# Lane 1's input product made by ScalarE and TensorE, both output products by GpSimd, in a selective-scan recurrence

## The chip, the cores and the metric

The kernel runs on one core of a Trainium2 chip. The metric is the device time of one launch in microseconds; lower is better.

## What is computed

Six sublayers of a post-norm decoder on x (4, 512, 128), each followed by a residual add and a LayerNorm: a long convolution (`hyena`), a masked cross attention (`cross0`), a quantised MLP (`bitffn`), a selective scan (`scan`), a cross attention with 16 heads (`cross1`) and a product-key mixture of 1024 experts (`experts`). The change touches the fourth, whose core is:

```python
u, res = split(x @ W_in)                       # (B, 512, 256) each
u = silu(u)
delta = softplus(u @ W_delta + b_delta)        # (B, 512, 256)
Bm = u @ W_B;  Cm = u @ W_C                    # (B, 512, 16) each
A = -exp(A_log)                                # (256, 16)
def step(h, inp):                              # over the 512 positions
    d_t, B_t, C_t, u_t = inp
    h = exp(d_t[..., None] * A) * h + d_t[..., None] * B_t[:, None, :] * u_t[..., None]
    return h, einsum('bdn,bn->bd', h, C_t)
y = (scan(step, 0, ...) + u * D_param) * silu(res)
return y @ W_out
```

For each state n of 16 and each sequence this is: an input product delta*u*B_n, a decay exp(delta*A_n), a first-order scan along the 512 positions, an output product h*C_n, and a sum over n.

## The kernel before

A hardware loop of two iterations takes two sequences each. The two are the *lanes* s = 0 and 1; each has its own arena in SBUF (`mem`, carved into tiles by `per_lane`) and its own four PSUM banks `ps[:, 0..3, :]`. Every engine has one program per sublayer and lane, written as a generator that yields stage numbers; `in_turn` merges the two lanes' generators by taking the smaller stage next, lane 0 first when equal. What comes out is one fixed instruction order for each engine. An engine that waits for a semaphore holds back all that stands behind it in this order; within one lane and engine the order is always that of the code. `w.next(G(name, s), k)` waits until the named semaphore has been raised k more times, `.then_inc` raises it, `w.link` waits for the engine's own instruction.

The recurrence holds its 256 channels as two halves of 128 partitions (DJ = 2), the 512 positions along the free dimension, so a tile of one n is 128 x 1024. Lane by lane, for n = 0 to 15:

- ScalarE (L964): the decay dA for n, two exponentials of 128 x 511; from n = 2 on after scan n - 2.
- TensorE (L682): B_n broadcast over the partitions into bank 0 by a matmul with `row_pick`, C_n likewise into bank 3. For this VectorE has split B and C into three bf16 parts (`BCS`, L1236 to L1240).
- VectorE, stage 4 + n (L1259): input product dBu = DU * B_n; stage 4.2 + n (L1267): the scan into HS or TU by turns.
- The output product HC: in lane 0 (`POOL_LANE = 0`) ScalarE copies C_n to SBUF (`CSB`) and GpSimd multiplies (L1479); in lane 1 VectorE multiplies (L1277).
- TensorE, stage 4.5 + n (L703): the sum over n, two matmuls with the identity that accumulate HC into banks 1 and 2.

Ahead of it lie, in stage 2, the products for delta (L671) and for B and C (L676), ScalarE's softplus as Abs, Exp (L952) and Ln (L955), and VectorE's delta (L1251) and DU = delta * u (L1254). Behind it lie VectorE's L1282 and L1286 (skip term and gate) and the output matmul (L710). GpSimd otherwise only makes the small inverse square roots (L1463) and, in the preparation, constants: among them `row_pick` (L362, L364), which stand ahead of `p_const`, for which TensorE's first matmul (L382) waits beside all the early loads (`p_load`, issued on SP and on ScalarE's queue). `bitffn`'s L1177 squares x on VectorE. SP's program only loads and stores.

Of the kernel before, what the change touches and what calls it, by code (L numbers as in the profile page):

```python
# [19 lines left out]
ALU = mybir.AluOpType  # L20
# [38 lines left out]
def decoder(nc, x, ctx_1024, mask_BxSxS2_ik1, L0_attn_w_in, L0_attn_b_in, L0_attn_w_conv,  # L59
# [28 lines left out]
    POOL_LANE = 0  # L88
# [3 lines left out]
    h_pad = nc.dram_tensor("h_pad", (3 * P,), F32, kind="Internal").ap()  # L92

    with ExitStack() as ctx:
# [18 lines left out]
        row_pick = sb("row_pick", [96, 2 * NS, P], BF16)  # L113
# [69 lines left out]
        WORDS = 12600  # L183
# [20 lines left out]
        def per_lane(**sizes):  # L204
# [16 lines left out]
        TU, TR, UU, SPA, SPE, DL, DU, BCS, BC1, BCM, dBu, HS, HC = per_lane(  # L221
            tu=(P, (DJ, S), F32), tr=(P, (DJ, S), F32), uu=(P, (DJ, S), F32), spa=(P, (DJ, S), F32),
            spe=(P, (DJ, S), F32), dl=(P, (DJ, S), F32), du=(P, (DJ, S), F32), bcs=(96, (S,), BF16),
            bc1=(2 * NS, (S,), F32), bcm=(2 * NS, (S,), BF16), dbu=(P, (DJ, S), F32), hs=(P, (DJ, S), F32),
            hc=(P, (2, DJ, S), F32))

        _, CSB = per_lane(front=(P, (7 * DJ * S + S // 2,), F32), csb=(P, (S,), F32))

        _, dA = per_lane(front=(P, (3 * DJ * S,), F32), da=(P, (2, DJ, S), F32))


# [39 lines left out]
            silu_r d_ready bc_ready ln_ready delta_ready bcs_ready B_ready C_ready dA_ready  # L271
            dbu_done scan_done hc_done y_acc yg_ready k_ready ksq_ready kn_ready kT_ready v_ready
            v_sb qsq_ready ssq_ready ssq_sb aq_sb s_drained xr_ready sim_ready sim_sb wh_ready wh_used
            z_ready g_sb hw_ready hwT_ready aq_ready own_done pn_ready wT_ready ssq_turned eo_ready eo_drained asum_ready c_sb softplus_step""".split()
# [64 lines left out]
        with nc.Block() as block:  # L339
# [15 lines left out]
            def _(pool):  # L355
# [6 lines left out]
                w.link(nc.gpsimd.memset(row_pick[:], 0.0))  # L362
                for g in range(3):
                    w.link(nc.gpsimd.affine_select(  # L364
                        out=row_pick[:], in_=row_pick[:], compare_op=ALU.not_equal, fill=1.0,
                        base=-2 * NS * g, pattern=[[-1, 2 * NS], [0, P]], channel_multiplier=1))
# [164 lines left out]
        def body(it):  # L531
            with nc.Block() as block:  # L532
                @block.sync
                def _(sp):
                    for s in range(LANES):
# [6 lines left out]
                                     .rearrange("o (k p) c -> p (o k) c", p=P)).then_inc(sg["mask_loaded"][s], 16)  # L542
                    for s in range(LANES):
# [13 lines left out]
        def pe_program(block):  # L557
            @block.tensor
            def _(pe):
# [96 lines left out]
                def scan(s):  # L656
# [23 lines left out]
                    def broadcast(row_n, bank, ready):  # L680

                        pe.matmul(ps[:, bank, :], row_pick[:, row_n, :], BCS[s][:], start=True, stop=True)\  # L682
                            .then_inc(G(ready, s), 1)

                    yield 3
                    w.next(G("bcs_ready", s))
                    w.next(G("delta_ready", s))
                    broadcast(0, 0, "B_ready")
                    broadcast(NS, 3, "C_ready")
                    for n in range(NS):  # L690
                        yield 4.1 + n
                        if n + 1 < NS:
                            w.next(G("dbu_done", s))
                            broadcast(n + 1, 0, "B_ready")
                        yield 4.5 + n
                        if n + 1 < NS and s == POOL_LANE:
                            w.next(G("c_sb", s))
                            broadcast(NS + n + 1, 3, "C_ready")
                        w.next(G("hc_done", s))
                        if n + 1 < NS and s != POOL_LANE:  # L700
                            broadcast(NS + n + 1, 3, "C_ready")
                        for j in range(DJ):
                            mm = pe.matmul(ps[:, 1 + j, :], ident[:], HC[s][:, n % 2, j, :],  # L703
# [824 lines left out]
```

## Time and profile before

| | us |
|---|---|
| median of 3 runs | 1267.41 |
| lowest and highest | 1264.33, 1274.64 |
| span of the profiled execution | 1266.5 |

| engine | busy us | share of the span | instructions |
|---|---|---|---|
| PE (TensorE matmul) | 885.7 | 70% | 3174 |
| DVE (VectorE) | 988.6 | 78% | 1819 |
| ACT (ScalarE) | 570.6 | 45% | 1593 |
| POOL (GpSimd) | 256.6 | 20% | 125 |

The two recurrences lie at 181 to 305 us and at 793 to 916 us. DVE is VectorE, PE is TensorE's matmuls and PEld its weight loads, ACT is ScalarE, POOL is GpSimd; L1267 is line 1267 of the kernel. A row of a timeline gives the start, the time from the start of its first to the end of its last instruction, the engine, the line, the operation, the tiles written and read, their shapes and how many instructions were merged (an f32 matmul of 512 columns leaves two records). In brackets stands the idle time before it and who ended it. A row of windows gives the stretch and its length, then the busy time and the instructions of PE, PEld, DVE, ACT and POOL, then the granted clock of TensorE as a share of 2.4 GHz, the share of the DMA engines and GB/s.

### The profile page before, as it was taken

What the parts mean: (1) busy time and instruction counts of PE and PEld (TensorE: products, weight loads), DVE (VectorE), ACT (ScalarE), POOL (GpSimd) and SP (SyncE); (2) the same over time, 40 slices, a digit from 0 to 9 for tenths busy, and PEclk for the clock granted to TensorE, in tenths of its full rate; (3) what the DMA queues carried; (4) which work ended last, traced back from release to release, by engine and by line L of the source; (5) the groups of instructions that cost most, each with busy time, mean ns of one, the idle gap of its engine ahead of it and who ended that gap; (6) DMA issues with size and microseconds to landing.
All of it is one profiled execution on the core that took longest, in us unless ns stands there. A gap on an engine that the chain in (4) does not pass through costs nothing. (4 is left out here: it accounts for less than half of the span.)

```text
span 1266.5 us, 10862 instructions
## 1 busy us (share of the span) xinstructions
PE 885.7 (70%) x3174; PEld 451.5 (36%) x3176; DVE 988.6 (78%) x1819; ACT 570.6 (45%) x1593; POOL 256.6 (20%) x125
## 2 busy tenths in 40 slices
PE   2551557767889868988826227676789996798893
PEld 1440312223346424444314112222243653344342
DVE  1278789998469579999816876999964975999993
ACT  1413353331434356865812146333333443966782
POOL 5011015554242010000000210555521501000000
PEclk9665578888989879999967568788899887999997
DMA  7100000000000000000010000000000000000000
GB/s 211 30 0 1 0 1 0 0 1 0 1 1 1 1 1 1 1 1 1 1 48 1 1 0 1 0 0 1 1 1 1 1 1 0 1 1 1 1 0 17
DMA packets 17403, 10.31 MB, mean 8 GB/s; under 512 B 6084, under 2 KB 16058, under 8 KB 17338
## 3 DMA queue, kind: packets, MB, share of 16 engines
q1 hardware_dynamic: 15368, 7.59, 2.2%
q10 hardware_dynamic: 1970, 1.97, 0.6%
q8 instruction: 27, 0.44, 0.1%
q14 instruction: 38, 0.31, 0.1%
HBM read 8.50 MB, written 1.05 MB: 8 GB/s over the span
## 5 line engine op out<-in xcount | busy, mean ns | idle before, releaser
L883 ACT ACTIVATE mem<-ps 77x512 f32<-77x512 f32 (+3 forms) x192 | 115.5, 603 | 387.4 <-POOL mem L1479 148.9
L1463 POOL TENSOR_TENSOR rs<-ve,minus_half 128x4 f32<-128x4 f32 (+2 forms) x60 | 102.0, 1709 | 811.5 <-DVE ve L1081 683.2
L851 PE MATMUL ps<-mem,ident 128*128 128x512 f32 x512 | 231.4, 600 | 30.5 <-DVE mem L1431 29.7
L1041 ACT ACTIVATE mem<-mem 128x32 f32<-128x32 f32 x1024 | 217.8, 308 | 0.0
L703 PE MATMUL ps<-mem,ident 128*128 128x512 f32 x256 | 154.9, 737 | 79.8 <-POOL mem L1479 79.8
L1479 POOL TENSOR_TENSOR mem<-mem 128x1024 f32<-128x1024 f32 x32 | 136.0, 4250 | 181.5 <-DVE mem L1267 181.5
L1431 DVE SCALAR_TENSOR_TENSOR mem<-mem 128x1024 f32<-128x1024 f32 x128 | 159.1, 1278 | 13.4 <-ACT mem L1041 12.0
L851 PEld LDWEIGHTS ps<-mem,ident 128*128 128x128 f32 x512 | 93.9, 190 | 167.1 <-issue 92.7
L1267 DVE TENSOR_TENSOR_SCAN mem<-mem 128x1024 f32<-128x1024 f32 x64 | 142.9, 2274 | 0.0
L1423 DVE TENSOR_TENSOR mem<-mem 128x1024 f32<-128x1024 f32 x96 | 112.9, 1216 | 0.3
L703 PEld LDWEIGHTS ps<-mem,ident 128*128 128x128 f32 x256 | 56.7, 233 | 157.1 <-POOL mem L1479 97.0
L964 ACT ACTIVATE mem<-mem,m_A 128x511 f32<-128x511 f32 x128 | 81.6, 709 | 1.1 <-DVE mem L1252 1.1
L1259 DVE TENSOR_TENSOR mem<-mem,ps 128x1024 f32<-128x1024 f32 x64 | 75.1, 1215 | 0.5 <-PE ps L682 0.4
L797 PE MATMUL ps<-mem 77*128 77x512 f32 x128 | 72.6, 656 | 0.0
L568 PE MATMUL ps<-ident,x 128*128 128x128 f32 x64 | 16.7, 412 | 62.6 <-DVE x L1088 31.6
L883 ACT ACTIVATE xT<-ps 128x512 f32<-128x512 f32 x20 | 11.9, 597 | 105.5 <-PE ps L568 102.8
L682 PE MATMUL ps<-mem,row_pick 96*128 96x512 bf16 x128 | 44.2, 426 | 19.5 <-DVE mem L1252 15.6
L792 PEld LDWEIGHTS ps<-ident,mem 128*77 128x77 f32 x256 | 36.9, 169 | 38.0 <-issue 26.8
L792 PE MATMUL ps<-ident,mem 128*77 128x128 f32 x256 | 45.2, 308 | 5.3 <-DVE mem L1348 5.3
L1312 DVE COPY mem<-ps 128x512 f32<-128x512 f32 x32 | 22.1, 692 | 32.7 <-PE ps L759 32.7
L780 PE MATMUL ps<-mem 64*128 64x77 f32 x512 | 38.9, 312 | 6.4 <-DVE mem L1330 6.4
L1111 DVE SCALAR_TENSOR_TENSOR mem<-mem,conv_w 128x511 f32<-128x511 f32 x8 | 6.0, 750 | 47.2 <-ACT mem L902 47.1
(223 smaller groups left out, 1269.9 us busy)
## 6 DMA issues: line engine op xcount, KB each, us to landing
x<-in_x_dram SPq DMA_DIRECT2D x4, 256.0 KB, 3.7
out_dram<-x SPq DMA_DIRECT2D x4, 256.0 KB, 2.3
mask<-in_mask_BxSxS_ik_dram SPq DMA_DIRECT2D x4, 154.0 KB, 3.5
mem<-n_L_ffn_expert_down_dram SPq DMA_DIRECT2D x1, 512.0 KB
mem<-in_L_xattn_Wo_dram SPq DMA_DIRECT2D x1, 512.0 KB
mem<-in_L_xattn_Wv_dram ACTq DMA_DIRECT2D x1, 512.0 KB
a_q<-in_L_xattn_Wq_dram SPq DMA_DIRECT2D x1, 512.0 KB, 4.4
a_k<-in_L_xattn_Wk_dram SPq DMA_DIRECT2D x1, 512.0 KB, 4.9
```

The source lines that it names most:

```text
L703: mm = pe.matmul(ps[:, 1 + j, :], ident[:], HC[s][:, n % 2, j, :], start=(n == 0), stop=(n == NS - 1), skip_group_check=True)
L792: mm = pe.transpose(ps[0:C, 2, k * P:(k + 1) * P], SC[s][:, j % GB, a, k, :], ident[:])
L851: mm = pe.matmul(ps[:, j, :], ident[:], WH[s][:, h % WB, j * 512:(j + 1) * 512], start=(h == 0), stop=(h == PH - 1), skip_group_check=True)
L883: ins = nc.scalar.activation(to, of, ACT.Copy, **kw)
L964: ins = nc.scalar.activation(dA[s][:, n % 2, j, 1:S], DL[s][:, j, 1:S], ACT.Exp, scale=m_A[:, j, n:n + 1])
L1041: ins = nc.scalar.activation(SVA[s][:, n % 2, i * NK:(i + 1) * NK], sims[:, 1, h, :], ACT.Identity, bias=sims[:, 0, h, i:i + 1])
L1259: nc.vector.tensor_tensor(dBu[s][:], DU[s][:], spread(ps[:, 0, :], 1, DJ), ALU.mult)\
L1267: nc.vector.tensor_tensor_scan(hs[:].rearrange(flat), dA[s][:, n % 2].rearrange(flat), dBu[s][:].rearrange(flat), 0.0, ALU.mult, ALU.add)\
L1423: nc.vector.tensor_tensor(sv.rearrange("p (i j) -> p i j", i=NK), spread(sims[:, 0, h, :], 2, NK), spread(sims[:, 1, h, :], 1, NK), ALU.add)\
L1431: nc.vector.scalar_tensor_tensor(out=WH[s][:, h % WB, :], in0=sv, scalar=TH[s][:, h:h + 1], in1=sv, op0=ALU.is_ge, op1=ALU.mult).then_inc( ...
L1463: nc.gpsimd.tensor_tensor(RS[s][0:rows, i * n:(i + 1) * n], VE[s][0:rows, i * n:(i + 1) * n], minus_half[0:rows, 0:n], ALU.pow)\
L1479: nc.gpsimd.tensor_tensor(HC[s][:, n % 2], (HS, TU)[n % 2][s][:], spread(CSB[s][:], 1, DJ), ALU.mult)\
```

## The change

Both output products are made by GpSimd; the VectorE branch for lane 1 goes. C_n comes from DRAM: ScalarE copies B and C (32 x 512) from PSUM to SBUF, SP writes them to a DRAM scratch and reads each row back over 128 partitions (256 KB), into two buffers CQ by turns. Lane 0 gets B_n the same way (BQ), and its input product is written to PSUM, banks 2 and 3 (`dbu`). In lane 1 (`BLEND_LANES`) TensorE turns DU once, ScalarE copies the result (`DUT`: positions on the partitions) and scales it for each n by a column of B, also turned (`BT`), into `DZ`, two buffers; TensorE turns DZ back into banks 2 and 3 with eight transposes a round. The scans of both lanes read this operand from PSUM. The sums move to banks 0 and 1. The bf16 split, the broadcast matmuls, `row_pick`, `CSB` and `dBu` go. Six semaphores more are cleared at an iteration's end. The core of the diff:

```diff
@@ pool_program, preparation
-                w.link(nc.gpsimd.memset(row_pick[:], 0.0))
-                for g in range(3):
-                    w.link(nc.gpsimd.affine_select(
-                        out=row_pick[:], in_=row_pick[:], compare_op=ALU.not_equal, fill=1.0, ...
@@ SP
+                    def broadcasts(s):
+                        w = Signals(sp)
+                        yield 0
+                        w.next(sg["bc_sb"][s])
+                        sp.dma_start(bc_rows[s], BCR[s][:]).then_inc(sg["bc_out"][s], 16)
+                        yield 0.5
+                        w.next(sg["bc_out"][s], 16)
+                        for n in range(NS):
+                            yield 1 + n
+                            slot = n % 2
+                            if s not in BLEND_LANES:
+                                if n >= 2:
+                                    w.next(sg["dbu_done"][s])
+                                sp.dma_start(BQ[s][:, slot, :], down(bc_rows[s][n, :]))\
+                                    .then_inc(sg[("B_even", "B_odd")[slot]][s], 16)
+                            if n >= 2:
+                                w.next(sg["hc_done"][s])
+                            sp.dma_start(CQ[s][:, slot, :], down(bc_rows[s][NS + n, :]))\
+                                .then_inc(sg[("C_even", "C_odd")[slot]][s], 16)
@@ TensorE, scan
+                    if s in BLEND_LANES:
+                        for k in range(NB):
+                            for j in range(DJ):
+                                mm = pe.matmul(ps[:, 0, k * NS:(k + 1) * NS], UU[s][:, j, k * P:(k + 1) * P],
+                                               m_bc[:, j, 0:NS], start=(j == 0), stop=(j == DJ - 1))
+                        mm.then_inc(G("bc_ready", s), 1)
+                        yield 2.8
+                        w.next(G("delta_ready", s), 2)
+                        w.next(G("bc_sb", s))
+                        for k in range(NB):
+                            for j in range(DJ):
+                                at = k % 2 * DI + j * P
+                                mm = pe.transpose(ps[:, 2 + k // 2, at:at + P], DU[s][:, j, k * P:(k + 1) * P], ident[:])
+                        mm.then_inc(G("turned", s), 1)
                     for n in range(NS):
-                        yield 4.1 + n
-                        if n + 1 < NS:
-                            w.next(G("dbu_done", s))
-                            broadcast(n + 1, 0, "B_ready")
+                        if s in BLEND_LANES:
+                            yield 3.7 + n
+                            w.next(G("dz_ready", s))
+                            if n == 0:
+                                w.next(G("xT_ready", s))
+                            else:
+                                w.next(G("scan_done", s))
+                            for j in range(DJ):
+                                for k in range(NB):
+                                    mm = pe.transpose(ps[:, 2 + j, k * P:(k + 1) * P],
+                                                      DZ[s][:, n % 2, k, j * P:(j + 1) * P], ident[:])
+                            mm.then_inc(G("dbu_done", s), 1)
                         yield 4.5 + n
-                        if n + 1 < NS and s == POOL_LANE:
-                            w.next(G("c_sb", s))
-                            broadcast(NS + n + 1, 3, "C_ready")
                         w.next(G("hc_done", s))
@@ ScalarE, scan
+                    w.next(G("bc_ready", s))
+                    copy(BCR[s][:], ps[0:2 * NS, 3, :], G("bc_sb", s))
+                    if s in BLEND_LANES:
+                        w.next(G("bc_ready", s))
+                        copy(BT[s][:].rearrange("p k n -> p (k n)"), ps[:, 0, 0:NB * NS], G("bc_sb", s))
                     yield 2.2
...
+                        if s in BLEND_LANES:
+                            if n == 0:
+                                yield 3.4
+                                turned(s, DUT[s][:].rearrange("p (a b) c -> p a (b c)", a=2), ps[:, 2:4, :], "xT_ready")
+                                act.wait_ge(G("xT_ready", s), XT_TURNS)
+                                w.next(G("bc_sb", s), 2)
+                            yield 3.5 + n
+                            if n >= 2:
+                                w.next(G("dbu_done", s))
+                            for k in range(NB):
+                                ins = nc.scalar.activation(DZ[s][:, n % 2, k, :], DUT[s][:, k, :], ACT.Identity,
+                                                           scale=BT[s][:, k, n:n + 1])
+                            ins.then_inc(G("dz_ready", s), 1)
@@ VectorE, scan
                     for n in range(NS):
-                        yield 4 + n
-                        w.next(G("B_ready", s))
-                        nc.vector.tensor_tensor(dBu[s][:], DU[s][:], spread(ps[:, 0, :], 1, DJ), ALU.mult)\
-                            .then_inc(G("dbu_done", s), 1)
+                        if s not in BLEND_LANES:
+                            yield 4 + n
+                            w.next(G(("B_even", "B_odd")[n % 2], s), 16)
+                            if n >= 1:
+                                w.next(G("scan_done", s))
+                            nc.vector.tensor_tensor(dbu, DU[s][:], spread(BQ[s][:, n % 2, :], 1, DJ), ALU.mult)\
+                                .then_inc(G("dbu_done", s), 1)
                         yield 4.2 + n
                         w.next(G("dbu_done", s))
                         w.next(G("dA_ready", s))
...
-                        yield 4.4 + n
-                        w.next(G("scan_done", s))
-                        w.next(G("C_ready", s))
-                        if n >= 2:
-                            w.next(G("y_acc", s))
-                        nc.vector.tensor_tensor(HC[s][:, n % 2], hs[:], spread(ps[:, 3, :], 1, DJ), ALU.mult)\
-                            .then_inc(G("hc_done", s), 1)
@@ GpSimd
-                    if s == POOL_LANE:
-                        for n in range(NS):
+                    for n in range(NS):
+                        yield 304.45 + n
+                        w.next(sg["scan_done"][s])
+                        w.next(sg[("C_even", "C_odd")[n % 2]][s], 16)
+                        if n >= 2:
+                            w.next(sg["y_acc"][s])
+                        nc.gpsimd.tensor_tensor(HC[s][:, n % 2], (HS, TU)[n % 2][s][:],
+                                                spread(CQ[s][:, n % 2, :], 1, DJ), ALU.mult)\
+                            .then_inc(sg["hc_done"][s], 1)
```

## Rows read from the trace of the kernel before

**Rows 1.** Page, first line: span of the profiled execution.

```profile
span 1266.5 us, 10862 instructions
```

**Rows 2.** Window over the first recurrence: stretch, length, busy us (instructions) by engine, clock.

```profile
180.00:308.00 128.00, 87.61 (x182) 33.76 (x183) 125.23 (x80) 45.14 (x75) 68.03 (x16) 0.83 0.00 0
```

**Rows 3.** Timeline, one round: start us, us, engine, line, operation, count.

```profile
228.80 4.46 DVE L1267 TENSOR_TENSOR_SCAN mem<-mem 128x1024 f32<-128x1024 f32 x2
...
231.16 4.26 POOL L1479 TENSOR_TENSOR mem<-mem 128x1024 f32<-128x1024 f32 x1 [3.64 <-DVE mem L1267]
...
233.30 1.22 DVE L1277 TENSOR_TENSOR mem<-mem,ps 128x1024 f32<-128x1024 f32 x1
234.44 2.34 DVE L1259 TENSOR_TENSOR mem<-mem,ps 128x1024 f32<-128x1024 f32 x2
...
235.47 3.78 PE L703 MATMUL ps<-mem,ident 128*128 128x512 f32 x4 [3.33 <-POOL mem L1479]
...
243.37 1.98 PE L703 MATMUL ps<-mem,ident 128*128 128x512 f32 x4 [0.40 <-POOL mem L1479]
```

**Rows 4.** Lines L1267 (scan), L1479 (output product): ns least/median/most.

```profile
L1267 DVE TENSOR_TENSOR_SCAN mem<-mem x64: 2261/2274/2285, 181.3 to 913.8; 128x1024 f32<-128x1024 f32 x64
...
L1479 POOL TENSOR_TENSOR mem<-mem x32: 4242/4249/4260, 183.6 to 914.0; 128x1024 f32<-128x1024 f32 x32
```

**Rows 5.** Timeline in bitffn: a GpSimd operation beside one of VectorE's.

```profile
105.23 0.68 DVE L1177 TENSOR_TENSOR r<-x 128x512 f32<-128x512 f32 x1
105.40 1.38 POOL L1463 TENSOR_TENSOR rs<-ve,minus_half 128x4 f32<-128x4 f32 x1 [3.54 <-DVE ve L1162]
...
107.51 1.01 POOL L1463 TENSOR_TENSOR rs<-ve,minus_half 128x4 f32<-128x4 f32 x1 [0.73 <-DVE ve L1162]
```

**Rows 6.** Windows: TensorE's granted clock around one fall.

```profile
200.30:203.90 3.60, 0.16 (x2) 0.04 (x1) 3.57 (x3) 0.00 (x0) 3.51 (x1) 1.00 0.00 0
204.00:207.40 3.40, 3.40 (x5) 1.22 (x6) 3.40 (x4) 2.94 (x5) 0.00 (x0) 0.52 0.01 2
```

**Rows 7.** Timeline, TensorE: four f32 transposes at either clock.

```profile
319.81 1.07 PE L568 MATMUL ps<-ident,x 128*128 128x128 f32 x4 [3.33 <-DVE x L1088]
...
324.58 0.60 PE L568 MATMUL ps<-ident,x 128*128 128x128 f32 x4
```

**Rows 8.** Timeline, head of the first recurrence.

```profile
167.13 1.90 PE L676 MATMUL ps<-mem,m_bc 128*32 128x512 f32 x4
...
167.94 1.28 ACT L952 ACT_TABLE_LOAD   x1
...
173.71 1.23 DVE L1251 TENSOR_TENSOR mem<-mem 128x1024 f32<-128x1024 f32 x1 [0.34 <-ACT mem L955]
...
177.75 1.23 DVE L1254 TENSOR_TENSOR mem<-mem 128x1024 f32<-128x1024 f32 x1
...
181.28 4.47 DVE L1267 TENSOR_TENSOR_SCAN mem<-mem 128x1024 f32<-128x1024 f32 x2
```

**Rows 9.** Timeline, end of the first recurrence.

```profile
304.96 1.22 DVE L1277 TENSOR_TENSOR mem<-mem,ps 128x1024 f32<-128x1024 f32 x1
...
311.72 1.40 DVE L1282 SCALAR_TENSOR_TENSOR mem<-mem,m_D,ps 128x512 f32<-128x512 f32 x2
...
311.86 2.05 PE L710 MATMUL ps<-m_out,mem 128*128 128x128 f32 x16 [1.04 <-DVE mem L1286]
```

**Rows 10.** Timeline, preparation, with the first layer's ScalarE scaling.

```profile
5.67 11.77 POOL L364 TENSOR_SCALAR_AFFINE_SELECT row_pick<-row_pick 96x4096 bf16<-96x4096 bf16 x3
...
20.97 0.34 PE L382 MATMUL ps<-f_t,f_w 3*64 3x1 f32 x2 [20.97 <-POOL f_row L374]
...
52.19 0.81 ACT L902 ACTIVATE mem<-mem,conv_b,conv_w 128x512 f32<-128x512 f32 x1
```

**Rows 11.** DMA, 17 to 18 us: ScalarE's queue.

```profile
q10 hardware_dynamic: 10, 0.02, 5.4%
```

**Rows 12.** Page, sixth part: a DMA of 256 KB, issue to landing.

```profile
x<-in_x_dram SPq DMA_DIRECT2D x4, 256.0 KB, 3.7
```

More of the change, by code:

```diff
@@ L87, in decoder @@
     GB = 3
-    POOL_LANE = 0
+    BLEND_LANES = (1,)
+    XT_TURNS = 6
     ACT_HEADS = (4, 7)
@@ L92, in decoder @@
     h_pad = nc.dram_tensor("h_pad", (3 * P,), F32, kind="Internal").ap()
+    bc_rows = [nc.dram_tensor(f"bc_rows{s}", (2 * NS, S), F32, kind="Internal").ap() for s in range(LANES)]
     with ExitStack() as ctx:
@@ L542, in _ @@
                                      .rearrange("o (k p) c -> p (o k) c", p=P)).then_inc(sg["mask_loaded"][s], 16)
+                    def broadcasts(s):
[17 more added lines that the diff above has]
+                                .then_inc(sg[("C_even", "C_odd")[slot]][s], 16)
+                    in_turn(broadcasts)
                     for s in range(LANES):
@@ L966, in scan @@
                         ins.then_inc(G("dA_ready", s), 1)
-                        if s == POOL_LANE:
-                            yield 3.6 + n
-                            w.next(G("C_ready", s))
-                            if n >= 1:
-                                w.next(G("hc_done", s))
-                            copy(CSB[s][:], ps[:, 3, :], G("c_sb", s))
+                        if s in BLEND_LANES:
[11 more added lines that the diff above has]
+                            ins.then_inc(G("dz_ready", s), 1)
                 def cross1(s):
@@ L1253, in scan @@
                     w.next(G("delta_ready", s))
-                    w.link(nc.vector.tensor_tensor(DU[s][:], DL[s][:], UU[s][:], ALU.mult))
+                    nc.vector.tensor_tensor(DU[s][:], DL[s][:], UU[s][:], ALU.mult).then_inc(G("delta_ready", s), 1)
                     flat = "p a b -> p (a b)"
+                    dbu = ps[:, 2:4, :]
+                    if s not in BLEND_LANES:
+                        w.next(G("delta_ready", s))
+                        w.next(G("bc_sb", s))
                     for n in range(NS):
-                        yield 4 + n
-                        w.next(G("B_ready", s))
-                        nc.vector.tensor_tensor(dBu[s][:], DU[s][:], spread(ps[:, 0, :], 1, DJ), ALU.mult)\
-                            .then_inc(G("dbu_done", s), 1)
+                        if s not in BLEND_LANES:
+                            yield 4 + n
[4 more added lines that the diff above has]
+                                .then_inc(G("dbu_done", s), 1)
                         yield 4.2 + n
@@ L1263, in scan @@
                         w.next(G("dA_ready", s))
[L1264 to L1265 removed]
+                        if n >= 2:
                             w.next(G("hc_done", s))
[L1267 to L1278 removed]
+                        nc.vector.tensor_tensor_scan((HS, TU)[n % 2][s][:].rearrange(flat),
+                                                     dA[s][:, n % 2].rearrange(flat), dbu.rearrange(flat), 0.0,
+                                                     ALU.mult, ALU.add).then_inc(G("scan_done", s), 1)
                     yield 5 + NS
[L1280 removed]
+                    w.next(G("y_acc", s), NS)
                     for j in range(DJ):
                         ins = nc.vector.scalar_tensor_tensor(out=TU[s][:, j, :], in0=UU[s][:, j, :],
[L1283 removed]
+                                                             scalar=m_D[:, j:j + 1], in1=ps[:, j, :],
                                                              op0=ALU.mult, op1=ALU.add)
```

62 lines of the change are left out of this document (12 added, 50 removed).

## The prediction

> **What bounds the kernel now.** I read the page first for the span, 1266.5 us [rows 1], then windows over each of the two recurrences, the stretch that the change rewrites. In the first of the two (the other is alike) VectorE is busy for 125.2 of 128 us, ScalarE for 45, GpSimd for 68, TensorE for 88 [rows 2]: VectorE sets the pace. The timeline says with what: one round holds two scans (4.46 us), one output product (1.22) and two input products (2.34) [rows 3], 8.0 in all. From the end of the first round's scans, 181.28 + 4.47 = 185.75 [rows 8], to the end of the last round's, where the next operation starts, 304.96 [rows 9], are 119.2 us for 15 rounds: 7.95 each. GpSimd's product and TensorE's sums lie beside this; nobody on VectorE waits for them.
>
> **Two prices that the rows hide.** First, GpSimd's product. It takes 4.24 to 4.26 us in all 32 cases [rows 4], and each time starts 0.1 us after lane 0's scan, just as lane 1's scan (2.27) begins. A scan here has two inputs in SBUF. What such a neighbour does is seen in [rows 5]: a GpSimd operation of 1.01 us takes 1.38 when it starts 0.17 us into VectorE's 0.68 us product x*x, also with two SBUF inputs. Of the 0.51 us left of that product 0.37 were added, so 0.14 of its start-up overlaps. So in the 4.25 us there are 2.27 - 0.1 - 0.14 = 2.03 of waiting and 2.22 of work. The bounds are 1.98 (4.25 - 2.27) and 4.25 (no waiting in it). I take 2.22, since [rows 5] shows the waiting. Second, TensorE's sum of one lane: 1.98 us at 2.4 GHz, 3.78 at 1.2 [rows 3]. Four f32 transposes take 0.60 or 1.07 [rows 7], so eight, at 0.11 or 0.21 for each further one (four f32 transposes less start-up), 1.03 or 1.92.
>
> The Trainium skill (SBUF — State Buffer, "Who interferes with whom") says that a VectorE instruction with two SBUF inputs and a GpSimd instruction that reads SBUF exclude each other, and that one SBUF input is harmless. By that rule the trace agrees: 1.38 beside 1.01.
>
> **The change, part by part.** *What goes.* VectorE loses lane 1's input product and output product: 2.4 us a round; left are one product and two scans, 1.2 + 4.5 = 5.8. The broadcasts on TensorE go too. The scans read one operand from PSUM, as L1259 and L1277 do at 1.22 us; L1251 with both in SBUF takes 1.23 [rows 8], so I leave the scan at 2.27 (nothing on VectorE is dearer from PSUM in these rows), and GpSimd is no longer held by it.
>
> *What sets the new pace.* Lane 1's own program on TensorE is: turn DZ(n) (stage 3.7 + n), then sum HC(n) (stage 4.5 + n), then turn DZ(n+1). Turning n+1 stands in the queue behind the sum of n, which waits for GpSimd's product of n; and the scan of n+1 waits for that turning. So lane 1 becomes a ring of four engines in which nothing overlaps, though DZ(n+1) has long been ready. Its stations from the end of scan n:
> GpSimd starts 0.1 later. At that moment VectorE has just begun lane 0's next input product, and this one reads DU and BQ, both in SBUF: GpSimd waits 1.22 - 0.1 - 0.14 = 0.98, then works 2.22: 3.2. To TensorE 0.05. Sum until the transposes can issue 1.8 (3.6 at 1.2 GHz; the 1.98 and 3.78 less the drain of the last). Eight transposes 1.03 (1.92). To VectorE 0.1. Scan 2.27.
> Sum: 8.55 at 2.4 GHz, 11.25 at 1.2. Lane 0 fits inside: product 1.22 and scan 2.27 end at 3.5, its GpSimd product at 5.8, its sum follows the transposes. ScalarE has per round four exponentials (2.54 before) and four scalings of 256 columns; one of 512 takes 0.81 [rows 10], so they lie between 0.4 and 0.81 each: at most 5.8 of 8.5. They are issued two rounds ahead, hidden.
>
> *The clock.* It was 0.83 on average [rows 2]. It fell after an idle stretch of 3.6 us and stayed at 1.2 GHz for 3.4 us of solid work [rows 6]; a mean of 0.83 is a third of the time, 44 of 128 us, at 1.2 GHz: 13 such stretches in 16 rounds, or fewer and longer ones. In the new ring TensorE works 1.98 + 1.03 + 1.8 and idles from the end of lane 0's sum (8.0) to the next (11.9): 3.9 us, a little more than now. So I expect a low stretch in half of the rounds or more. One of 3.4 us costs the ring 1.8 (the sum), one twice as long 2.7. Between 8.55 and 11.25 I take 9.7; now the clock costs nothing, since VectorE covers it.
>
> The Trainium skill (TensorE: Matmul & The Clock Gate, Part 4) says that transposes do not count as activity for the clock. If so the clock would fall in nearly every round, which by the rows above is 10.3 us a round; no row here has transposes alone for long enough to tell.
>
> *Head.* VectorE loses five operations that split B and C into bf16, but its next step waits for ScalarE's logarithm anyway (0.34 us idle before L1251 [rows 8]). ScalarE gains copies of B and C and, in lane 1, one that waits for 16 more small matmuls. These follow the bc matmuls, which end at 167.13 + 1.90 = 169.03, and are bound by their weights, like the 16 records of L710 in 2.05 us [rows 9]: 171.0, copy to 171.4. Only then can the exponential's table load start, now at 167.94: 3.45 late. DU of lane 1 is then ready at 177.75 + 1.23 + 3.45 = 182.4. Then a serial start: eight transposes at the low clock 1.9, a copy of 1024 columns 1.1 (at most twice the 0.81), four scalings 2.0, eight transposes 1.9, steps between 0.2, scan 2.27: 191.8, against 185.75: **+6.1** (5 to 7.5).
>
> *Tail.* Now lane 1's last steps start 311.72 - 304.96 = 6.8 after the last scan, because both sums queue. In the new order lane 0 is done by then and lane 1 needs 0.1 + 2.2 + 0.05 + 1.98 = 4.4: **-2.4**.
>
> *The DMAs.* Three of 256 KB a round; such a one lands in 3.7 us [rows 12]. C(n) of lane 1 is issued when product n-2 is done, 3.3 us into a ring that began two rounds earlier, so it has 2 x 9.7 - 3.3 = 16 us. SP has nothing else to do in that time. The first ones (one write, then reads, some 8 us from 170) are there before 182. Cost nothing; cover gone only beyond 16 us.
>
> *Preparation.* Setting row_pick up goes: 11.77 us and a memset before it, ahead of the p_const that releases TensorE at 20.97 [rows 10]. ScalarE's load queue still moves its last packets in 17 to 18 us [rows 11], so the loads, not GpSimd, release TensorE then, near 18.5: between 0 and 3.5 gained, I take **-2.5**. Six more semaphores to clear per iteration: +1 in all, within the 15 us between iterations.
>
> **Sum.** Two recurrences of 15 rounds: 2 x (6.1 - 2.4 + 15 x (9.7 - 7.95)) - 2.5 + 1 = 2 x 29.95 - 1.5 = +58. On 1266.5 this is 1325; the median of the runs, 1267.4, is 0.9 above that execution, so 1326.
>
> **Rivals.**
> 1. *The ring at the high clock* (8.55 a round): 2 x (3.7 + 9.0) - 1.5 = +24, 1291. For it: the mean clock was 0.83. Against: a longer idle stretch than now. 12%.
> 2. *The ring mostly at the low clock* (10.3 to 11.25): 2 x (3.7 + 35.3) - 1.5 = +77 at 10.3, 1344; +105, 1372, at 11.25. 13%.
> 3. *GpSimd's 4.25 us is its own* (or a scan from PSUM holds it as well). Then 1.05 more a round and 2 at each tail: +94, 1361. Against: [rows 5]. 7%.
> 4. *VectorE's product does not hold GpSimd*: 7.6 at the high clock, and TensorE's idle stretch shrinks to 2.3 us, so the clock might stay high: 2 x (3.7 - 5.3) - 1.5 = -5, 1263: no change. Against: that product is of the very kind in [rows 5]. 5%.
> 5. *The other side: VectorE stays the bound.* Its sum is 5.8 a round; if turning n+1 did not wait for sum n, the round would be set by VectorE or by TensorE, at 5.8 to 6.5: 2 x (3.7 - 15 x 1.8) - 1.5 = -48, near 1219 at 6.15. It decides from a ring under 7.3 us, where the gain passes 1%. Against it stands the order of yields, and that the ring's least is 0.1 + 1.98 + 0.05 + 1.8 + 1.03 + 0.1 + 2.27 = 7.3 even with nothing in GpSimd's way. 3%.
> My forecast, the ring at 8.9 to 10.3: 60%.
>
> **Range.** The forecast's own is 1302 to 1344. For 8 in 10 I add rival 1 below and most of 2 and 3 above: 1288 to 1368. A measurement of this kernel tells apart some 1%, 13 us. Faster 3% (rival 5), within it 6% (rival 4 and a lucky ring), slower 91%.
>
> **What the profile after would show.** Scans of a lane 8.6 to 11 us apart and VectorE idle before lane 1's scan, waiting for TensorE; TensorE idle before the lane 1 sum, waiting for GpSimd; lane 0's product on GpSimd near 2.2 us (beside a scan that reads PSUM) and lane 1's near 3.2 us (beside VectorE's product); both 4.25 would be rival 3, both 2.2 rival 4. The first scan of lane 1 ending some 6 us later after DU. TensorE in preparation starting near 18.5. The forecast is wrong if VectorE is busy throughout the recurrence, if a scan from PSUM is dearer than 2.27 (each 0.1 costs 3 us), or if GpSimd waits for C rows.

## The result

| | before | changed |
|---|---|---|
| median us | 1265.87 (4 runs) | 1342.43 (4 runs) |
| lowest, highest | 1261.69, 1274.64 | 1337.38, 1343.56 |
| span of the profiled execution | 1266.5 | 1335.7 |

The ratio of the changed kernel to the one before is 1.059, with an interval of 1.055 to 1.064: slower, by 77 us. The prediction was 1326 with 1288 to 1368.

The recurrence of the changed kernel. First the two lines that answer to [rows 4], the scan and GpSimd's product (least/median/most ns), and VectorE's product:

```profile
L1301 DVE TENSOR_TENSOR_SCAN mem<-mem,ps x64: 2286/2287/2289, 178.0 to 983.8; 128x1024 f32<-128x1024 f32 x64
```

```profile
L1503 POOL TENSOR_TENSOR mem<-mem x64: 2342/2358/3252, 180.3 to 986.1; 128x1024 f32<-128x1024 f32 x64
```

```profile
L1294 DVE TENSOR_TENSOR ps<-mem x32: 1206/1209/1226, 176.7 to 975.8; 128x1024 f32<-128x1024 f32 x32
```

Then one round of the timeline, which answers to [rows 3]. The MATMUL lines of L722 are the eight transposes; of L728 the one at 242.88 is lane 0's sum, the one at 248.75 lane 1's:

```profile
242.01 1.04 PE L722 MATMUL ps<-ident,mem 128*128 128x128 f32 x8
...
242.88 1.88 PE L728 MATMUL ps<-mem,ident 128*128 128x512 f32 x4
243.08 2.29 DVE L1301 TENSOR_TENSOR_SCAN mem<-mem,ps 128x1024 f32<-128x1024 f32 x1 [4.52 <-PE ps L722]
...
245.28 1.21 DVE L1294 TENSOR_TENSOR ps<-mem 128x1024 f32<-128x1024 f32 x1
...
245.45 3.25 POOL L1503 TENSOR_TENSOR mem<-mem 128x1024 f32<-128x1024 f32 x1 [4.46 <-DVE mem L1301]
246.53 2.29 DVE L1301 TENSOR_TENSOR_SCAN mem<-mem,ps 128x1024 f32<-128x1024 f32 x1
...
248.75 3.67 PE L728 MATMUL ps<-mem,ident 128*128 128x512 f32 x4 [3.99 <-POOL mem L1503]
...
252.26 1.04 PE L722 MATMUL ps<-ident,mem 128*128 128x128 f32 x8
...
253.33 2.29 DVE L1301 TENSOR_TENSOR_SCAN mem<-mem,ps 128x1024 f32<-128x1024 f32 x1 [4.52 <-PE ps L722]
```

From the end of lane 1's scan (243.08 + 2.29) the reader can walk the ring: GpSimd's product of lane 1, 245.45 to 248.70; TensorE's sum of lane 1, from 248.75 at the low clock; behind it in the same queue the eight transposes at 252.26; the next scan of lane 1 at 253.33, 10.25 us after the one before. VectorE sat idle for 4.5 us ahead of it. The granted clock around one fall (columns as in [rows 6]) and over the whole recurrence:

```profile
244.80:248.70 3.90, 0.00 (x0) 0.00 (x0) 3.87 (x3) 2.93 (x6) 3.25 (x1) 1.00 0.00 0
248.75:252.10 3.35, 3.35 (x4) 1.41 (x5) 0.06 (x1) 1.33 (x2) 2.35 (x1) 0.50 0.47 153
252.30:255.00 2.70, 2.70 (x13) 1.41 (x11) 1.67 (x1) 0.00 (x0) 0.00 (x0) 1.00 0.39 102
```

```profile
180.00:338.00 158.00, 97.62 (x252) 45.33 (x252) 88.46 (x48) 64.96 (x124) 86.65 (x32) 0.83 0.21 69
```

VectorE's busy time went from 125 us of 128 to 88 of 158, against [rows 2]: VectorE has less work now, and the ring sets the pace.

How often the clock falls can be read from TensorE's idle time ahead of lane 1's sums. In both recurrences of the changed kernel 14 such stretches are 3.6 to 4.0 us long, and 13 of the 14 are followed by a sum of 3.7 us; the one of 3.58 is followed by a sum at the high clock:

```profile
199.16 1.98 PE L728 MATMUL ps<-mem,ident 128*128 128x512 f32 x4 [3.58 <-POOL mem L1503]
```

The kernel before already showed nearly the same. In each of its recurrences the idle stretch ahead of a round's first sum was 3.3 us or more in 8 of the 16 rounds, and all 8 were followed by a slowed sum (2.4 to 3.8 us); in the rounds between them it was at most 2.3 us, and the sum took 1.98. Two of them in a row:

```profile
203.86 3.67 PE L703 MATMUL ps<-mem,ident 128*128 128x512 f32 x4 [3.44 <-POOL mem L1479]
...
211.77 1.98 PE L703 MATMUL ps<-mem,ident 128*128 128x512 f32 x4 [1.66 <-POOL mem L1479]
```

The head, answering to [rows 8], and the tail, answering to [rows 9]:

```profile
161.67 1.90 PE L694 MATMUL ps<-mem,m_bc 128*32 128x512 f32 x4
...
163.51 1.96 PE L701 MATMUL ps<-m_bc,mem 128*128 128x16 f32 x16
...
165.75 1.28 ACT L982 ACT_TABLE_LOAD   x1
...
176.83 1.97 PE L710 MATMUL ps<-ident,mem 128*128 128x128 f32 x8 [11.37 <-DVE mem L1282]
...
181.65 1.97 PE L722 MATMUL ps<-ident,mem 128*128 128x128 f32 x8 [2.85 <-ACT mem L1007]
...
183.66 2.29 DVE L1301 TENSOR_TENSOR_SCAN mem<-mem,ps 128x1024 f32<-128x1024 f32 x1 [3.42 <-PE ps L722]
```

```profile
335.25 2.29 DVE L1301 TENSOR_TENSOR_SCAN mem<-mem,ps 128x1024 f32<-128x1024 f32 x1 [4.50 <-PE ps L722]
...
337.62 2.34 POOL L1503 TENSOR_TENSOR mem<-mem 128x1024 f32<-128x1024 f32 x1 [4.45 <-DVE mem L1301]
...
342.97 1.41 DVE L1307 SCALAR_TENSOR_TENSOR mem<-mem,m_D,ps 128x512 f32<-128x512 f32 x2 [1.93 <-PE ps L728]
```

And the preparation, against [rows 10]: GpSimd no longer releases TensorE, a load on ScalarE's queue does.

```profile
18.10 0.37 PE L378 MATMUL ps<-f_t,f_w 3*64 3x1 f32 x2 [18.10 <-DMA mem<-in_L_xattn_Wv_dram]
```

Where the 69 us between the two profiled spans are, with the terms of the sum beside them:

| term | predicted | measured | from |
|---|---|---|---|
| a round of the ring | 9.7 | 10.11 | end of lane 1's scans, 185.95 to 337.54, 15 rounds |
| 2 x 15 rounds against 7.95 | +52.5 | +64.8 | |
| head, from lane 1's bc matmuls to its first scan's end | +6.1 | +5.7 | 161.67 to 185.95 against 167.13 to 185.75 |
| tail, last scan's end to lane 1's last steps | -2.4 | -1.3 | 337.54 to 342.97 against 6.8; the sum took 2.92, part of it at the low clock |
| preparation | -2.5 | -2.9 | TensorE's first matmul at 18.10 in place of 20.97 |
| semaphores, two ends of an iteration | +1 | +1.1 | last store's issue to next load's: 15.65 in place of 15.08, taken twice |

The rows are from the first recurrence, and the second is alike to within 0.5 us. Two heads and tails taken, these make +71.8. The remaining -2.6 lies between TensorE's first matmul and lane 1's bc matmuls of the first recurrence, mostly in layers that the change does not touch. From that first matmul to GpSimd's last operation ahead of the recurrence (142.04 in the changed kernel) the traces of all the kernels here spread over 4.9 us, though these layers are the same in them; why is not shown.

### The profile page after: what moved, and what is told of

Its sections match the earlier page's. It is cut to its first block and busy times, and to the rows that moved or that the text cites. A ratio compares the mean times of both kernels' runs of the same rounds, so it can differ in the third digit from the quotient of the medians.

```text
span 1335.7 us, 11403 instructions
## 1 busy us (share of the span) xinstructions
PE 909.3 (68%) x3350; PEld 481.4 (36%) x3352; DVE 909.8 (68%) x1735; ACT 613.4 (46%) x1697; POOL 282.8 (21%) x153
## 5 line engine op out<-in xcount | busy, mean ns | idle before, releaser
L728 PE MATMUL ps<-mem,ident 128*128 128x512 f32 x256 | 174.7, 820 | 121.5 <-POOL mem L1503 121.5
L876 PE MATMUL ps<-mem,ident 128*128 128x512 f32 x512 | 231.4, 600 | 30.6 <-DVE mem L1456 29.8
L1301 DVE TENSOR_TENSOR_SCAN mem<-mem,ps 128x1024 f32<-128x1024 f32 x64 | 146.3, 2287 | 139.1 <-PE ps L722 138.0
L1503 POOL TENSOR_TENSOR mem<-mem 128x1024 f32<-128x1024 f32 x64 | 177.2, 2769 | 216.5 <-DVE mem L1301 216.5
L908 ACT ACTIVATE mem<-ps 77x512 f32<-77x512 f32 (+6 forms) x168 | 101.3, 605 | 249.8 <-PE ps L817 69.4
L994 ACT ACTIVATE mem<-mem,m_A 128x511 f32<-128x511 f32 x128 | 84.8, 712 | 151.3 <-DVE mem L1301 150.1
L728 PEld LDWEIGHTS ps<-mem,ident 128*128 128x128 f32 x256 | 58.1, 252 | 196.2 <-POOL mem L1503 149.4
L1007 ACT ACTIVATE mem<-mem 128x256 f32<-128x256 f32 x128 | 54.1, 493 | 0.1
L722 PEld LDWEIGHTS ps<-ident,mem 128*128 128x128 f32 x256 | 35.1, 161 | 37.4 <-issue 30.9
L805 PEld LDWEIGHTS ps<-mem 64*128 64x128 f32 x512 | 36.3, 222 | 14.8 <-issue 7.6
```

The costliest lines, as they stand in the source:

```text
L728: mm = pe.matmul(ps[:, j, :], ident[:], HC[s][:, n % 2, j, :], start=(n == 0), stop=(n == NS - 1), skip_group_check=True)
L805: mm = pe.matmul(ps[:, a, k * C:(k + 1) * C], AQ[s][a * E:(a + 1) * E, j, k * P:(k + 1) * P], KT[s][a * E:(a + 1) * E, j, :], start=True, ...
L876: mm = pe.matmul(ps[:, j, :], ident[:], WH[s][:, h % WB, j * 512:(j + 1) * 512], start=(h == 0), stop=(h == PH - 1), skip_group_check=True)
L908: ins = nc.scalar.activation(to, of, ACT.Copy, **kw)
L994: ins = nc.scalar.activation(dA[s][:, n % 2, j, 1:S], DL[s][:, j, 1:S], ACT.Exp, scale=m_A[:, j, n:n + 1])
L1301: nc.vector.tensor_tensor_scan((HS, TU)[n % 2][s][:].rearrange(flat), dA[s][:, n % 2].rearrange(flat), dbu.rearrange(flat), 0.0, ALU.mult, ...
```

## The experiments

**1. Turn ahead of the sum.** In lane 1's TensorE program the turning of DZ(n+1) goes ahead of the sum of n; the waits are the same.

```diff
+                    if s in BLEND_LANES:
+                        yield 3.7
+                        turn_back(0)
                     for n in range(NS):
-                        if s in BLEND_LANES:
-                            yield 3.7 + n
-                            ...                     # waits and eight transposes for n
+                        if s in BLEND_LANES and n + 1 < NS:
+                            yield 4.3 + n
+                            turn_back(n + 1)
                         yield 4.5 + n
```

> The changed kernel, with lane 1's turning of DZ(n+1) on TensorE ahead of the sum of n instead of behind it. Ring theory (the turning waited in TensorE's queue for a sum that waited for GpSimd): the ring opens, VectorE is the bound at 5.8 us a round (one product, two scans), so scans of a lane lie 5.9 to 6.5 us apart instead of 10.1; 30 rounds of 4 us less: about 1342 - 120 = 1222 us, faster than the kernel before. Rival, GpSimd with two products a round and its holds is the bound by itself: it works 2.35 + 3.25 = 5.6 us a round, so this rival gives a round of 5.6 at least too, but more if VectorE's product now meets both of its products: up to 7.5, 1265 us. Rival, the order is not what costs (latency between engines, clock): rounds above 9, over 1300 us.

Measured: 1209.95 us, ratio to before 0.957 (0.954 to 0.959), 132 us less than the changed kernel and 12 us less than expected. Two rounds of its timeline, scans of both lanes merged, and the windows row:

```profile
245.06 5.65 POOL L1509 TENSOR_TENSOR mem<-mem 128x1024 f32<-128x1024 f32 x2 [0.20 <-DVE mem L1307]
...
247.07 1.43 DVE L1300 TENSOR_TENSOR ps<-mem 128x1024 f32<-128x1024 f32 x1
...
247.30 1.06 PE L720 MATMUL ps<-ident,mem 128*128 128x128 f32 x8 [0.41 <-DVE mem L1307]
...
248.54 4.46 DVE L1307 TENSOR_TENSOR_SCAN mem<-mem,ps 128x1024 f32<-128x1024 f32 x2
...
254.38 2.29 DVE L1307 TENSOR_TENSOR_SCAN mem<-mem,ps 128x1024 f32<-128x1024 f32 x1
```

```profile
200.00:260.00 60.00, 49.24 (x171) 22.88 (x170) 59.66 (x32) 43.75 (x82) 58.04 (x22) 1.00 0.44 138
```

The transposes start at 247.30, 0.15 us after the end of lane 1's scan, and are over before VectorE has finished lane 0's product; scans are 5.85 us apart; VectorE is busy for 59.7 of 60 us, GpSimd for 58.0, and TensorE, busy with the same matmuls in less time, is granted 1.00. So the whole loss, and the gain that the change holds, hung on the place of eight transposes in one queue. The rival of GpSimd as a bound by itself is nearly true too: 5.65 of 5.85. VectorE's 1.43 us for lane 0's product, 1.21 in the changed kernel, contain a short wait, since it starts while GpSimd is still at lane 0's output product.

**2. The clock.** Ten matmuls with zero weights fill TensorE's idle stretch in the ring of the changed kernel; they add zero to lane 1's sum.

```diff
                         yield 4.5 + n
+                        if s in BLEND_LANES and n >= 1:
+                            for _ in range(10):
+                                pe.matmul(ps[:, 0, :], zero_w[:], q1T[:], start=False, stop=False, ...)
                         w.next(G("hc_done", s))
```

> The changed kernel, with ten bf16 matmuls of 512 columns with zero weights that add nothing to lane 1's sum, ahead of TensorE's wait for lane 1's product in each round from the second on (2.1 us at 2.4 GHz, 4.3 at 1.2, in the 4 us in which TensorE idles). Clock theory (the low clock lengthens lane 1's sum by 1.7 us in 14 of 15 rounds): the granted clock stays at 1.00 through the recurrence, the sum takes 1.98 in place of 3.67, rounds 8.6 in place of 10.1: about 1342 - 46 = 1296 us. Rival, the clock falls anyhow or the added work delays the sum: rounds of 10.1 or more, no gain. Under the rival that the rounds' length does not hang on the sum, the clock is high and the time stays.

Measured: 1291.06 us, ratio to before 1.021 (1.016 to 1.026). The filler, the sum behind it and the next two scans of lane 1:

```profile
243.57 2.29 DVE L1307 TENSOR_TENSOR_SCAN mem<-mem,ps 128x1024 f32<-128x1024 f32 x1 [2.84 <-PE ps L724]
...
245.09 2.32 PE L730 MATMUL ps<-q1T,zero_w 128*128 128x512 bf16 x10
...
249.25 1.98 PE L734 MATMUL ps<-mem,ident 128*128 128x512 f32 x4 [1.83 <-POOL mem L1509]
...
252.14 2.29 DVE L1307 TENSOR_TENSOR_SCAN mem<-mem,ps 128x1024 f32<-128x1024 f32 x1 [2.83 <-PE ps L724]
```

```profile
200.00:330.00 130.00, 100.98 (x403) 49.95 (x402) 88.72 (x74) 50.98 (x96) 77.65 (x30) 0.99 0.23 74
```

The clock stays up (0.99), the sum takes 1.98 us in place of 3.67, and a round 8.57. That is the ring that the prediction worked out for the high clock, 8.55. The kernel is 51 us faster than the changed one; 30 rounds of 8.57 in place of 10.11 make 46 of them. So some two thirds of the loss were the clock's, and more work on TensorE made the kernel faster. What is left of the loss, 25 us against the kernel before, is the ring at the high clock with its head and tail; rival 1 of the prediction had put it at 24.

**3. The turned lane left out.** `BLEND_LANES = ()`: both input products on VectorE, from rows of B by DMA.

> The change without its turned lane: both lanes' input products by VectorE from rows of B that come by DMA, written to PSUM; both output products by GpSimd. Ring theory: no ring; VectorE's sum, 2 x 1.21 + 2 x 2.29 = 7.0 us, sets the round, with GpSimd near it (one product meets both of VectorE's, 2.35 + 2.2, the other is free, 2.35: 6.9). Rounds 7.0 to 7.6 against 7.95 before and 10.1 in the changed kernel; the serial start of lane 1 goes too: about 1342 - 2 x (15 x 2.9 + 5) = 1245 us, faster than before by 1.5 to 2.5 percent. Rival, four DMAs of 256 KB a round come late: VectorE waits for B rows and rounds are above 8.

Measured: 1296.67 us, ratio to before 1.024 (1.021 to 1.027); 52 us above what was expected, and not by the rival's cause (late DMAs) either. One round:

```profile
241.05 4.45 DVE L1301 TENSOR_TENSOR_SCAN mem<-mem,ps 128x1024 f32<-128x1024 f32 x2
...
243.40 5.62 POOL L1503 TENSOR_TENSOR mem<-mem 128x1024 f32<-128x1024 f32 x2 [3.36 <-PE ps L728]
245.42 4.69 DVE L1294 TENSOR_TENSOR ps<-mem 128x1024 f32<-128x1024 f32 x2
...
250.03 4.45 DVE L1301 TENSOR_TENSOR_SCAN mem<-mem,ps 128x1024 f32<-128x1024 f32 x2
```

```profile
L1294 DVE TENSOR_TENSOR ps<-mem x64: 1224/1417/3370, 175.9 to 937.1; 128x1024 f32<-128x1024 f32 x64
```

Rounds are 8.98 us, with no ring (VectorE never idles in the round) and no late DMA. VectorE's two products take 4.69 us instead of 2.4: the first one starts while GpSimd's lane 0 product is at work (243.40 to 245.75), then GpSimd's second is held by the first, and VectorE's second by GpSimd's second; one lasts up to 3.37 us. I had counted the hold on GpSimd's side alone. So the turned lane is worth having, once its order is that of experiment 1 (1210 us); in the order of the change it was the worse of the two (1342 against 1297). It takes one of the instructions with two SBUF inputs off VectorE.

**4. Lane 0's product to SBUF.** In the changed kernel, so that lane 0's scan has two SBUF inputs again (`DB` is a new SBUF tile).

```diff
-                    dbu = ps[:, 2:4, :]
+                    dbu = ps[:, 2:4, :] if s in BLEND_LANES else DB[s][:]
```

> The changed kernel, with lane 0's input product written to SBUF instead of PSUM, so that lane 0's scan reads two operands from SBUF again; lane 1 is as it was. Theory (a VectorE instruction with two SBUF inputs shuts GpSimd's product out for its length): lane 1's product on GpSimd, which meets VectorE's product and now lane 0's scan behind it, goes from 3.25 to about 5.5 us, and the ring by the same 2.2 us a round: +67 us, about 1409; lane 0's product stays at 2.35. If GpSimd gets in between the two VectorE instructions, it stays near 3.25 and the scan is held instead, which lies off the ring: no change. Rival, the 4.25 us before the change had another reason: GpSimd's 3.25 and 2.35 stay and the scan starts right behind the product; no change.

Measured: 1334.19 us, ratio to before 1.050 (1.044 to 1.056). That is 8 us under the changed kernel, with intervals that just overlap (its own is 1.055 to 1.064), so a small gain is neither shown nor excluded; the loss of 67 us that the first theory named is excluded. The scans by their operands:

```profile
L1303 DVE TENSOR_TENSOR_SCAN mem<-mem x32: 2291/4316/4324, 178.2 to 973.9; 128x1024 f32<-128x1024 f32 x32
L1303 DVE TENSOR_TENSOR_SCAN mem<-mem,ps x32: 2285/2287/2289, 183.9 to 980.7; 128x1024 f32<-128x1024 f32 x32
```

The scan with both operands in SBUF takes 4.32 us and the one with one in PSUM 2.29: GpSimd's product got in between VectorE's product and the scan, and the scan stood still for 2.03 us. Of the outcomes named this is the second. The exclusion is real and works both ways, and here it fell on lane 0's scan, which lies off the ring, so the time hardly moved: from the fifth round of the first recurrence on, rounds are 10.25 us as in the changed kernel. The rival (no exclusion) falls: the same line of code takes 2.03 us more with its operand in SBUF. It also fits GpSimd's 4.25 us before the change [rows 4], where the scan came first: with the scans' operand in PSUM they are 2.35.

**5. Moving the hold off the ring.** Three kernels, each the changed one with an instruction on VectorE ahead of lane 0's product, which lets GpSimd's lane 1 product start first: a memset of 256 columns, one of 640, and a reduction of 128 x 512 with one input.

```diff
                                 w.next(G("scan_done", s))
+                                nc.vector.memset(nap[:], 0.0)     # in the third: tensor_reduce(nap[:, 0:NB], X[s][:], AX.X, ALU.add)
                             nc.vector.tensor_tensor(dbu, DU[s][:], spread(BQ[s][:, n % 2, :], 1, DJ), ALU.mult)
```

> The changed kernel as it was (ring of 10.1 us), with a memset of a spare tile of 256 columns (some 0.2 to 0.3 us) ahead of lane 0's input product on VectorE, so that GpSimd's lane 1 product starts first. Theory (whoever starts first shuts the other out for its whole length, and GpSimd's wait of 0.9 us lies on the ring, VectorE's does not): GpSimd's lane 1 product falls from 3.25 to 2.35, VectorE's lane 0 product grows from 1.21 to about 3.1, rounds are 0.9 us shorter: 1342 - 27 = 1315 us; if TensorE's shorter idle stretch also keeps its clock up, up to 1.7 more a round, down to 1270. Rival, the hold is symmetric in its price or VectorE's delay reaches the ring through lane 0's scan: no gain, 1342 or above.

> As e7, with the spare tile 640 columns wide, so that VectorE's lane 0 product starts 0.7 us after the scan instead of 0.27. In e7 GpSimd's product started 0.11 us before VectorE's and was held all the same (3.51 us). Theory: GpSimd reads SBUF only some 0.15 us after its start; with 0.5 us of lead it gets in: 2.35 us in place of 3.25, VectorE's product grows to about 3 us, and the ring is 0.9 us shorter: about 1342 - 27 = 1315 us, less if TensorE's idle stretch (3 us in place of 4) now keeps its clock at 2.4 GHz. Rival, VectorE's instruction has the right of way whenever it comes: GpSimd takes 4 us, the round grows by 0.4 or more: 1350 and above.

> As e8, with the memset of the spare tile replaced by a reduction of 128 x 512 of x (one input in SBUF, 0.69 us in this kernel's profile) into a spare tile. In e7 and e8 GpSimd's product was held until 2.19 us before its end, that is to the end of VectorE's product, although it had started 0.1 and 0.5 us ahead of it. Theory A: the memset itself holds GpSimd, so GpSimd never had the start; behind a reduction with one input it gets in: 2.35 us in place of 3.25, VectorE's product grows to about 3 us, the ring is 0.9 shorter, about 1315 us. Theory B: VectorE's instruction has the right of way even when it comes 0.5 us later: GpSimd takes about 4 us and the time is 1355 to 1365 as in e8.

Measured: 1338.29 us (ratio to before 1.056, 1.054 to 1.058), 1362.11 (1.075, 1.070 to 1.080) and 1278.90 (1.011, 1.007 to 1.015). First the memset of 640, then the reduction:

```profile
246.54 3.91 POOL L1505 TENSOR_TENSOR mem<-mem 128x1024 f32<-128x1024 f32 x1 [4.44 <-DVE mem L1303]
246.55 0.59 DVE L1295 MEMSET nap<- 128x640 f32 x1
247.06 1.21 DVE L1296 TENSOR_TENSOR ps<-mem 128x1024 f32<-128x1024 f32 x1
```

```profile
238.63 0.66 DVE L1295 TENSOR_REDUCE nap<-x 128x4 f32<-128x512 f32 x1
...
238.79 2.36 POOL L1505 TENSOR_TENSOR mem<-mem 128x1024 f32<-128x1024 f32 x1 [0.58 <-DVE mem L1303]
...
239.20 3.03 DVE L1296 TENSOR_TENSOR ps<-mem 128x1024 f32<-128x1024 f32 x1
...
253.34 2.29 DVE L1303 TENSOR_TENSOR_SCAN mem<-mem,ps 128x1024 f32<-128x1024 f32 x1 [0.63 <-PE ps L723]
```

```profile
L1505 POOL TENSOR_TENSOR mem<-mem x64: 2337/2350/2367, 182.3 to 932.4; 128x1024 f32<-128x1024 f32 x64
```

Behind the memset GpSimd is held although it started 0.5 us ahead of VectorE's product: 3.91 us, ending 2.2 after the product's end. It had started together with the memset. Behind the reduction it is free, 2.34 to 2.37 in all 64 cases, and VectorE's product waits instead (3.03). So the right of way goes to the first, and a memset on VectorE holds GpSimd like an instruction with two SBUF inputs. With GpSimd's 0.9 us off the ring TensorE idles for 1 to 3 us ahead of a sum instead of 4, and its clock rises to 0.91:

```profile
200.00:300.00 100.00, 65.15 (x192) 30.58 (x190) 95.82 (x48) 50.69 (x96) 56.14 (x24) 0.91 0.29 94
```

Rounds are now 8.0 and 8.9 us by turns, 8.4 on average against 10.1. VectorE is busy for 95.8 of 100 us, its wait for GpSimd included, so it has nearly become the bound in place of the ring. The expectation of 1315 had only the 0.9 us, 27 us in 30 rounds. Of the other 36 us the shorter rounds make 23, and these fit the rise of the clock, which the expectation of e7 had named. In the two profiled executions another 11 us lie behind the recurrences, in layers that none of the edits touches; no run says why. The first of the three kernels told nothing by itself, and the second left two readings open: that the memset holds GpSimd, or that VectorE's product takes the right of way even when it comes later. The third decided for the memset, with a lead (0.41 us) no longer than the second's.

**6. Two further steps from experiment 1.** The head: lane 1's copies on ScalarE no longer stand ahead of the exponentials.

```diff
-                    w.next(G("bc_ready", s))
-                    copy(BCR[s][:], ps[0:2 * NS, 3, :], G("bc_sb", s))
-                    if s in BLEND_LANES: ...        # waits for BT's matmuls and copies it
+                    if s not in BLEND_LANES: ...    # lane 0's copy to BCR stays here
                     yield 2.2
                     ...                             # Exp
+                    if s in BLEND_LANES: ...        # the copy to BCR; BT's copy goes to stage 3.4
```

> The reordered kernel (turning ahead of the sum, 1210 us) with one more edit in the head of each recurrence: lane 1's copy of B and C on ScalarE moves behind its exponential, and the copy of the turned B, which waited for 16 small matmuls ahead of the exponentials, moves to just before DUT is copied. Theory (these waits put the exponential's table load off by about 3 us in each of two heads, as part of the head's +5.7): the table load starts 3.2 us earlier after lane 1's last Abs, VectorE's first DL step likewise: 2 x 3.2 less, about 1203.5 us. Rival, lane 1's serial start (turn, copy, scale, turn back) hides it: no change; or lane 1's rows of C now come late for the first product: no change or slightly slower.

Measured: 1201.14 us, ratio to before 0.948 (0.945 to 0.951), 9 us under experiment 1 where 6.5 was expected; its six runs spread over 9 us themselves:

```profile
165.84 1.90 PE L694 MATMUL ps<-mem,m_bc 128*32 128x512 f32 x4
...
166.65 1.28 ACT L986 ACT_TABLE_LOAD   x1
```

The table load starts 0.8 us after lane 1's bc matmuls start, in place of 4.1 in the changed kernel (165.75 after 161.67). From those matmuls to the end of lane 1's first scan it is 21.5 us instead of 24.3 in experiment 1, so two heads make 5.6 us of the 9. This is the fastest version of the study. And both lanes turned (`BLEND_LANES = (0, 1)` on experiment 1, not on the earlier head):

> The reordered kernel (1210 us) with both lanes' input products made by ScalarE and TensorE, so that VectorE has two scans a round (4.5 us) and no instruction with two SBUF inputs in the recurrence, and GpSimd works 2 x 2.35 = 4.7 unheld. Bounds by the rows: ScalarE 2.54 + 2 x 1.69 = 5.9 us a round, TensorE at 2.4 GHz 2 x (1.72 + 0.86) = 5.2. If only the fullest engine counts, rounds of 5.9 to 6.2 as now (5.85) and 3 to 8 us more at the heads: 1213 to 1225. Rival, chains between the engines (exponentials queue behind scalings) lengthen the round to 7 or more: above 1240. Other rival, VectorE's freedom wins: rounds under 5.6, below 1200.

Measured: 1209.72 us, ratio to before 0.952 (0.949 to 0.956): the same as experiment 1, with another bound.

```profile
200.00:260.00 60.00, 58.55 (x267) 35.40 (x266) 49.11 (x22) 60.00 (x129) 50.11 (x23) 1.00 0.31 95
```

ScalarE is busy for all of 60 us (two exponentials a lane and 8 scalings a round), VectorE for 49. Rounds are 5.60 us on average (one of 7.2, then five of 5.2 to 5.3, then 5.64), 0.24 less than in experiment 1; the head is 2 us longer, and VectorE waits 7 us for TensorE in it. The time is 3 us under the expected range, and VectorE's freedom did not bring it below 1200.

## Why the prediction was right

- **What bounds the kernel before** and the prices hidden in the rows: right. GpSimd's product alone was put at 2.22 us and takes 2.34 to 2.36; held by VectorE's product it was put at 3.2 and takes 3.25. The scan from PSUM was left at 2.27 and takes 2.29.
- **The ring**: right in its cause, shown by experiment 1, and in its length at the high clock, 8.55 against 8.57 in experiment 2. This carried the sign. The size it carried only in part: the ring at the high clock is worth 25 us (experiment 2 against before), the clock the other 51, in the forecast 24 and 35.
- **The clock**, the term that was mis-sized. Between 8.55 and 11.25 I took 9.7; the rounds were 9.84, 8.56 and then 13 of 10.25. The step that failed is "a low stretch in half of the rounds or more": the idle stretch was 3.9 to 4.0 us, as worked out, and each of the 13 of that length was followed by a fall. The mean clock of 0.83 hid this. Before the change a long idle stretch came only in every second round, but each of them was followed by a fall, so the rows of before spoke for a fall in nearly every round of a ring with 3.9 us of idle time. The price of one fall was right (1.7 against 1.8), so the rounds sit at rival 2's lower edge, 10.3. That is 12 us of recurrence; the median came out 16 us above the forecast, the profiled span 11 us above its own sum. The Trainium skill (TensorE: Matmul & The Clock Gate, Part 4) says that transposes do not count as activity for the clock, for which the prediction had worked out the same 10.3. No run here shows that this is the reason, and in experiment 1 the same transposes stand in a stretch granted 1.00.
- **Head, tail, preparation**: +5.7, -1.3 and -2.9 against +6.1, -2.4 and -2.5. The tail gained less than forecast because its sum took 2.92 us in place of 1.98, part of it at 1.2 GHz.
- **DMAs**: right that they cost nothing; 96 of them landed in 3.4 us (median), and nobody waited for one in the ring.
- **Rival 5**, VectorE as the bound with rounds of 5.8 to 6.5 and a kernel near 1219, is what experiment 1 made: 5.85 and 1210. The prediction gave it 3% because of the order of yields, and that was the reason it did not come.
- Slips in the prediction's working that moved nothing: rival 4 puts TensorE's idle stretch at 2.3 us, but 3.9 less the 0.98 that it takes off is 2.9; and its least ring of 7.3 us would be 7.7, since GpSimd's product takes 2.35 and not the lower bound of 1.98.
- Rival 3 (GpSimd's 4.25 us its own) and rival 4 (VectorE's product does not hold it) fell with the first rows of the new profile.

## What to carry to other kernels

When a lane's product of round n+1 is moved onto an engine that also closes round n, look at what stands ahead of it in that engine's queue: here a turning whose input had long been ready waited behind a sum that waited for two other engines, and four engines ran in a ring (10.1 us) though at the high clock none had more than 5.8 us of work. Read the clock stretch by stretch and not from its mean: how long the idle stretch is, and what the next work behind it costs. Work out the ring at both clocks of TensorE, since a ring that leaves it idle also slows its share of the ring. And count the exclusion between GpSimd and VectorE in both directions, then let it fall on the one that is off the path.

## What the runs showed that was not expected

- The hold works in both directions, first come, first served: the scan with two SBUF inputs took 4.32 us in place of 2.29 behind GpSimd's product, and VectorE's product up to 3.37 in place of 1.21. Without a ring at all this made the change slower than the kernel before (1297 us).
- A memset on VectorE (592 ns for 640 columns) holds GpSimd's product; a reduction with one SBUF input (0.66 us) does not.
- Added matmuls with zero weights, 2.3 us in each of 30 rounds, took 51 us off the changed kernel, 46 of them in rounds that are shorter because TensorE's clock stays at 2.4 GHz.
